# Routed expert slots of a vision-transformer block: up and down matmuls interleaved by chunk, one register load per slot, gathers issued earlier

## The chip, the cores and the metric

The kernel runs on one core of a Trainium2 chip. The metric is device time in microseconds for one execution. A core has five engines that run their own instruction streams and meet at semaphores: PE (matmul; its weight loads are listed as PEld), DVE (elementwise, reductions), ACT (activations, copies), POOL (here gathers, scatters and small arithmetic) and SP (here DMA starts). In the views below PEldq stands for instructions that PE's sequencer carries out itself, such as address arithmetic.

## What is computed

```python
h = tok(x)                                    # patches @ W.T + b, 32 images x 36 patches, width 256
h = concatenate([cls_tok, h])                 # 37 tokens per image, 1184 in all
h = h + attn(layernorm(h))                    # 4 heads, plus a memory read, out projection
...
# ffn(layernorm(h)): one shared expert, and the two best of 8 routed experts
shared = silu(x @ shared_w1.T) @ shared_w2.T                  # 256 -> 1024 -> 256
gate_logits = x @ gate_w.T
top_k_gates, top_k_idx = top_k(gate_logits, 2); top_k_gates = softmax(top_k_gates)
h_e = einsum('td,ehd->teh', x, experts_w1)
expert_out = einsum('teh,edh->ted', silu(h_e), experts_w2)
return h + shared + einsum('ted,te->td', expert_out, gates)
```

## The kernel before

**Stages.** The tokens stand in 11 tiles of 111 (three images each). A front part embeds them and runs attention, software-pipelined over 16 steps. Then comes the shared expert, tile by tile, and meanwhile DVE works out where each token goes. Last come the routed experts as 26 *slots* (`SLOT_TILES`) of 128 rows, each slot for one expert; the rest of this text is on the slots. A tile or slot has a running number `n`, slot `j` being `n = NT + j` with `NT = 11`.

**Precision.** Tokens, hidden values and weights are each split into a high and a low fp16 part, and three products are summed.

**One slot on PE.** `turn` (L559) transposes the slot's gathered rows (4 matmuls, L563) into one PSUM bank. `up` (L567) makes the 1024 hidden values in 8 chunks of 128, each chunk from 6 matmuls of 128 columns (L577, 48 in all); after chunk 3 and chunk 7 it signals `hid_ready` for a half. `down` (L584) brings them back to 256 values: 8 chunks of two matmuls, one of 512 columns (L592) and one of 256 (L594), summed into one bank; it waits for `lo_ready` before chunk 0 and before chunk 4. The weights of all experts lie in SBUF, and which expert a slot uses is known only at run time, so the address of each matmul's weights is computed from a register `base_of[j]`. Four address instructions per `up` chunk and one per `down` chunk, 40 per slot, stand in PE's stream between the matmuls; the order view prints them as ISA, the trace as FUSED_REGOPS.

**Registers.** `know` (L633) fills the registers with one TENSOR_LOAD (L625) of 13 values of `expert_of` (`LOADED = 13`): once before slot 0, and once within slot 12's step, behind its `up`.

**One step.** `slot_step(j)` (L650) has: `up` of slot j, `turn` of slot j+1 (`rows_of`, L637), `down` of slot j-1. For the first slots it also waits until DVE has prepared the weights of the experts that may be needed (`wait_split`).

**The other engines, per slot.** ACT: two `silu` activations (L800, a half each), then `copy_x_t` (L791), which brings the turned rows of the next slot to SBUF, where the next `up` needs them (`x_t_ready`), then up to two conversions of late weight chunks (L730). DVE: `split_hidden` (L1203 high part, L1205 low part, for each half), then `output` of slot j-1 (L1212, L1215: scale by the gate, add the two halves of the bank), then the low part of late weight chunks (L1042; two each in slots 0 to 3, one in 4 and 5). POOL: wait for the slot's result (`y_scaled`) and for the scatter before it (`added`), scatter-add the result to the output (L935), then gather the rows of slot j+4 (L896). Scatters are strictly one after another, since they add into the same rows.

All streams are written out by hand in this order; no scheduler moves anything.

Of the kernel before, what the change touches and what calls it, by code (L numbers as in the profile page):

```python
# [18 lines left out]
ACT = mybir.ActivationFunctionType  # L19
# [6 lines left out]
P = 128  # L26
IMAGES, SEQ, D = 32, 37, 256
PER_TILE = 3
T = PER_TILE * SEQ
NT = -(-IMAGES // PER_TILE)  # L30
# [21 lines left out]
def build(nc, patches, w_embed, embed_bias, w_qk, w_v, w_o, out_bias, betas, mem, z, w_ffn, w_gate,  # L52
# [3 lines left out]
    with ExitStack() as ctx:  # L56
# [233 lines left out]
        def wait_split(eng, chunks):  # L290

            eng.wait_ge(w_lo, chunks)
# [78 lines left out]
        def _(pe):  # L371
# [251 lines left out]
            def experts(first):  # L623

                return nc.values_load_multi_w_load_instructions(  # L625
                    expert_of[0:1, first:min(first + LOADED, SLOT_TILES)],
                    engines=[mybir.EngineType.PE], min_val=EW, max_val=EXPERTS * EW,
                    skip_runtime_bounds_check_because="an expert's number is clamped to 1..EXPERTS where "
                                                      "expert_of is written")[1]

            base_of = {}

            def know(first):  # L633
                for i, value in enumerate(experts(first)):
                    base_of[first + i] = value
# [8 lines left out]
            know(0)  # L644
            wait_split(pe, 2 * CHUNKS)
# [3 lines left out]

            def slot_step(j, r, quad_next):  # L650
# [15 lines left out]
        def _(act):  # L666
# [125 lines left out]

            def silu(n, b, m, first=False):
                for half_ in range(2):
                    act.wait_ge(hid_ready, 2 * n + half_ + 1)
                    if not first:
                        act.wait_ge(lo_ready, 2 * n + half_ - 1)
                    d_ = act_out[:, half_].rearrange("p (a b) -> p a b", b=P)[:, :, 0:m]
                    s_ = bank[2 * b + half_][:].rearrange("p (a b) -> p a b", b=P)[:, :, 0:m]
                    nc.scalar.activation(d_, s_, ACT.Silu,  # L800
                                         scale=1.0 / (X_SCALE * W_SCALE)).then_inc(hid_acted, 1)
# [23 lines left out]
            late_hi(NT - 1)  # L825
            for j in range(len(LATE_SLOT) + len(LATE_SLOT) % 2):
                silu(NT + j, (NT + j) % 2, P)
                copy_x_t(NT + j + 1, (NT + j + 1) % 2, P)
                late_hi(NT + j)
            with act.Fori(len(LATE_SLOT) // 2 + len(LATE_SLOT) % 2, (SLOT_TILES - 2) // 2) as i:  # L830
                for r in range(2):
                    n = 2 * i + r + NT
                    silu(n, (NT + r) % 2, P)
                    copy_x_t(n + 1, (NT + r + 1) % 2, P)
            n = NT + (SLOT_TILES - 2) // 2 * 2
            for n in range(n, NT + SLOT_TILES):
                silu(n, n % 2, P)
                if n + 1 < NT + SLOT_TILES:
                    copy_x_t(n + 1, (n + 1) % 2, P)

        @block.gpsimd
        def _(pool):
# [88 lines left out]
            for j in range(SLOT_TILES):  # L931
                pool.wait_ge(y_scaled, NT + j + 1)
# [5 lines left out]
                if j + 4 < SLOT_TILES:  # L938
                    gather(j + 4)
# [406 lines left out]
```

## Time and profile before

| | us |
|---|---|
| median of 3 runs | 401.28 (400.87 to 401.45) |
| the profiled execution, its own time | 397.15 |
| its span, first to last instruction | 395.4 |
| front part and shared expert, up to slot 1's first matmul | 233.1 |
| slot 1's first matmul to slot 25's first | 141.25 (24 steps) |
| from there to the end of the span | 21.0 |

PE is busy 337.2 us (85%), DVE 255.3, ACT 164.4, POOL 162.3. Busy PE is not PE at its peak: a matmul's recorded duration overlaps the next one's, so starts are to be read, not durations. The chain of waits is the list, in order of time, of what each piece of the last work waited for; "issue" in it is time for which the profile shows no wait.

### The profile page before, as it was taken

Reading aid. Unit: us, or ns where it says so; the run is one execution under the profiler, and the core shown is the slowest. Engines: PE = TensorE matmul, PEld = TensorE weight load, DVE = VectorE, ACT = ScalarE, POOL = GpSimd, SP = SyncE. Lnnn points to the kernel's source line nnn. Section 1 sums busy time; section 2 is a strip of 40 time slices with the busy share of each in tenths; the row PEclk is TensorE's granted clock in tenths of the full one; section 3 lists DMA queues with packets and bytes.
Section 4 is the critical chain, followed back from the end, with each engine's and each line's share of the span. In section 5 each row is a group of like instructions: output and inputs, shape, how many; then the busy total and the mean of one; then the engine's idle time right before and its main releaser. Section 6 shows DMA issues by size and latency. Waiting matters only on the chain.

```text
span 395.4 us, 9873 instructions
## 1 busy us (share of the span) xinstructions
PE 337.2 (85%) x3430; PEld 278.8 (71%) x3430; DVE 255.3 (65%) x559; ACT 164.4 (42%) x371; POOL 162.3 (41%) x232
## 2 busy tenths in 40 slices
PE   4488989889887775499899999999996999999970
PEld 3367878778876563488788788688874887788740
DVE  0156778878684845489998679885563656665640
ACT  1036665675656533534344456542221322332210
POOL 0246575657651212004814312654442444544331
PEclk9699999999996856599999999999998999999995
DMA  7553233343222210634356637322331233323321
GB/s 247 167 183 137 94 98 88 118 130 135 77 78 65 63 37 27 215 121 81 111 118 172 159 87 228 44 47 51 55 56 27 31 54 55 46 39 53 41 28 13
DMA packets 18401, 36.32 MB, mean 92 GB/s; under 512 B 3349, under 2 KB 11000, under 8 KB 18360
## 3 DMA queue, kind: packets, MB, share of 16 engines
q1 hardware_dynamic: 11992, 27.71, 21.9%
q0 software_dynamic: 6368, 8.03, 13.7%
q8 instruction: 29, 0.48, 0.5%
q14 instruction: 12, 0.10, 0.1%
HBM read 28.52 MB, written 7.21 MB: 90 GB/s over the span
## 4 chain that ended last, share of the span: by engine, by line
PE 56%; DVE 17%; POOL 9%; issue 6%; ACT 5%; DMA 5%; SPq 1%; DVEq 0%; POOLq 0%; ACTq 0%
PE bank L577 21%; PE bank L592 13%; PE bank L594 7%; PE bank L454 3%; POOL weights L857 3%; PE bank L491 3%; PE bank L434 2%; DVE weights L1042 2%; DMA weights<-in_out_bias 2%; DVE hid_lo L1205 2%; PE bank L563 2%; PE bank L472 2%; PE bank L462 2%; ACT weights L730 2%; DVE weights L980 2%
## 5 line engine op out<-in xcount | busy, mean ns | idle before, releaser
L577 PEld LDWEIGHTS bank<-x_t,weights 128*128 (+1 forms) x1776 | 102.9, 99 | 8.8 <-issue 1.7
L577 PE MATMUL bank<-x_t,weights 128*128 128x128 f16 (+1 forms) x1776 | 107.3, 220 | 2.0 <-ACT x_t L791 1.9
L592 PE MATMUL bank<-weights,hid_hi 128*128 (+1 forms) x296 | 99.7, 384 | 2.1 <-DVE hid_lo L1205 1.7
L800 ACT ACTIVATE act_out<-bank 128x512 f32<-128x512 f32 (+1 forms) x74 | 42.8, 580 | 128.9 <-PE bank L577 115.3
L594 PE MATMUL bank<-weights,hid_lo 128*128 (+1 forms) x296 | 81.3, 275 | 0.0
L935 POOL DMA_INDIRECT out_rows<-y,add_id x26 | 42.6, 1640 | 79.7 <-DVE y L1215 72.1
L592 PEld LDWEIGHTS bank<-weights,hid_hi 128*128 128x128 f16 (+1 forms) x296 | 32.1, 109 | 31.3 <-issue 1.9
L1205 DVE SCALAR_TENSOR_TENSOR hid_lo<-act_out,hid_hi 128x512 f16<-128x512 f32 (+1 forms) x74 | 50.8, 687 | 2.5
L1203 DVE TENSOR_SCALAR hid_hi<-act_out 128x512 f16<-128x512 f32 (+1 forms) x74 | 37.0, 500 | 23.1 <-ACT act_out L800 22.3
L1042 DVE SCALAR_TENSOR_TENSOR weights<-stage,weights 128x1024 f16<-128x1024 f32 x36 | 43.7, 1227 | 2.4 <-ACT weights L730 2.4
L434 PE MATMUL bank<-weights 128*111 128x256 f32 x132 | 33.2, 405 | 5.6 <-DMA weights<-in_w_embed 5.6
L730 ACT ACTIVATE weights<-stage 128x1024 f16<-128x1024 f32 x36 | 37.4, 1055 | 0.0
L856 POOL TENSOR_SCALAR weights<-weights 111x1 f32<-111x1 f32 x22 | 5.0, 230 | 71.3 <-DVE weights L963 70.9
L594 PEld LDWEIGHTS bank<-weights,hid_lo 128*128 128x128 f16 (+1 forms) x296 | 32.2, 109 | 2.3
L1212 DVE TENSOR_SCALAR y<-bank,slot_gate 128x256 f32<-128x256 f32 x26 | 12.6, 484 | 32.2 <-PE bank L594 31.0
L434 PEld LDWEIGHTS bank<-weights 128*111 128x111 f32 x132 | 24.2, 191 | 11.0 <-DMA weights<-in_w_embed 5.6
L896 POOL DMA_INDIRECT slot_rows<-x_rows,gather_id x26 | 27.7, 1065 | 7.9 <-issue 4.9
L923 POOL DMA_DIRECT2D out_rows<-y x11 | 10.2, 928 | 49.7 <-DVE y L1215 49.7
L454 PE MATMUL bank<-weights 128*128 128x111 f32 x176 | 24.0, 293 | 7.7 <-ACT weights L683 7.6
L454 PEld LDWEIGHTS bank<-weights 128*128 128x128 f32 x176 | 22.2, 204 | 9.3 <-ACT weights L683 8.9
L857 POOL TENSOR_TENSOR weights<-weights 111x1 f32<-111x1 f32 x22 | 24.3, 1107 | 1.8
L791 ACT COPY x_t<-bank 128x512 f16<-128x512 f16 (+1 forms) x37 | 20.9, 564 | 4.1 <-PE bank L563 4.1
(130 smaller groups left out, 448.4 us busy)
## 6 DMA issues: line engine op xcount, KB each, us to landing
stage<-in_w_ffn SPq DMA_DIRECT2D x36, 512.0 KB, 4.7
weights<-in_patches SPq DMA_DIRECT2D x11, 333.0 KB, 3.0
x_rows<-rows SPq DMA_DIRECT2D x11, 111.0 KB
out_rows<-weights SPq DMA_DIRECT2D x10, 111.0 KB
out_rows<-y POOLq DMA_DIRECT2D x10, 111.0 KB, 3.1
weights<-in_w_embed SPq DMA_DIRECT2D x1, 768.0 KB, 4.4
weights<-in_w_qk SPq DMA_DIRECT2D x1, 512.0 KB
slot_rows<-x_rows,gather_id POOLq DMA_INDIRECT x26
```

The source lines that it names most:

```text
L434: mm = nc.tensor.matmul(bank[4][0:T, 0:D], s_patch[:, t % 2, k], s_we[:, k], start=(k == 0), stop=(k == PC - 1))
L454: mm = nc.tensor.matmul(bank[5][:, o * T:(o + 1) * T], s_wqk[:, k, o], xln_t[:, t % 2, k], start=(k == 0), stop=(k == KC - 1))
L577: mm = nc.tensor.matmul(o, weights[:, bass.ds(base + 2 * k * CHUNK + 2 * (col - col % D) + w * D + col % D, P)], x_t[:, b, (2 * x + k) * P ...
L592: nc.tensor.matmul(bank[5 + b][0:m, :], hid_hi[:, b, c * P:c * P + m], weights[:, bass.ds(at, 2 * D)], start=(c == 0), stop=False)
L594: mm = nc.tensor.matmul(bank[5 + b][0:m, 0:D], hid_lo[:, b, c * P:c * P + m], weights[:, bass.ds(at, D)], start=False, stop=(c == HC - 1))
L730: nc.scalar.mul(hi_of(c), staged_of(c), W_SCALE).then_inc(w_hi, 1)
L800: nc.scalar.activation(d_, s_, ACT.Silu, scale=1.0 / (X_SCALE * W_SCALE)).then_inc(hid_acted, 1)
L857: link(nc.gpsimd.tensor_tensor(y_, v_, half[0:T, 0:1], ALU.pow))
L935: nc.gpsimd.indirect_dma_start(out=out, out_offset=bass.IndirectOffsetOnAxis(ap=add_id[:, j:j + 1], axis=0), in_=y[:, (NT + j) % 2], in_of ...
L1042: nc.vector.scalar_tensor_tensor(out=lo_of(c), in0=staged_of(c), scalar=W_SCALE, in1=hi_of(c), op0=ALU.mult, op1=ALU.subtract).then_inc(w_ ...
L1203: nc.vector.tensor_scalar(four(hid_hi), src, H_SCALE, None, ALU.mult).then_inc(hi_ready, 1)
L1205: nc.vector.scalar_tensor_tensor(out=four(hid_lo), in0=src, scalar=H_SCALE, in1=four(hid_hi), op0=ALU.mult, op1=ALU.subtract).then_inc(lo_ ...
```

## The change

On PE a slot step no longer runs all of `up`, then `turn`, then all of `down`. It runs up chunk c of slot j, then down chunk c of slot j-1, for c from 0 to 7 (`up_chunk`, `down_chunk`), with `turn` of slot j+1 and the register load of slot j+1 between up chunk 4 and down chunk 4. `know` loads one value: two loads before slot 0, then one in each of the steps 1 to 24. On ACT the copy of the next slot's rows stands between the two activations of a slot instead of behind them, with the weight conversions behind the second. On POOL the gather of slot j+4 stands ahead of the wait for slot j's result. DVE and SP are as before.

```diff
-LOADED = 13
...
+            def know(j):
+
+                base_of[j] = nc.values_load_multi_w_load_instructions(
+                    expert_of[0:1, j:j + 1], engines=[mybir.EngineType.PE], min_val=EW, max_val=EXPERTS * EW,
...
             know(0)
+            know(1)
             wait_split(pe, 2 * CHUNKS)
             up(NT, NT % 2, P, base_of[0])
             rows_of(1, 1, 0)
             down(NT - 1, 0, T, 0)
...
             def slot_step(j, r, quad_next):
 
+                this_expert, last_expert = base_of[j], base_of[j - 1]
                 if j < EXPERTS:
                     wait_split(pe, (j + 2) * CHUNKS)
-                up(NT + j, (NT + r) % 2, P, base_of[j])
-                if (j + 1) % LOADED == 0 and j + 1 < SLOT_TILES:
-                    know(j + 1)
-                if quad_next is not None:
-                    rows_of(j + 1, (r + 1) % 4, quad_next)
-                down(NT + j - 1, (NT + r + 1) % 2, P, base_of[j - 1])
+                n, b = NT + j, (NT + r) % 2
+                pe.wait_ge(x_t_ready, n + 1)
+                for c in range(HC):
+                    up_chunk(n, b, P, this_expert, c)
+                    if c == 4 and quad_next is not None:
+                        rows_of(j + 1, (r + 1) % 4, quad_next)
+                        know(j + 1)
+                    down_chunk(n - 1, 1 - b, P, last_expert, c)
...
+            def slot_act(n, b):
+                silu_half(n, b, P, 0)
+                copy_x_t(n + 1, 1 - b, P)
+                silu_half(n, b, P, 1)
...
             for j in range(SLOT_TILES):
+                if j + 4 < SLOT_TILES:
+                    gather(j + 4)
                 pool.wait_ge(y_scaled, NT + j + 1)
                 if j:
                     pool.wait_ge(added, 16 * j)
                 nc.gpsimd.indirect_dma_start(
...
-                if j + 4 < SLOT_TILES:
-                    gather(j + 4)
```

PE, before, in the step of slot 12: the end of its `up` (L577), the load of 13 values, the turning of slot 13's rows, and the start of `down` of slot 11.

```order
L577 ISA
L577 MATMUL bank<-x_t,weights 128x128
L625 TENSOR_LOAD expert_of
L563 MATMUL bank<-id,slot_rows 128x128 [waits slot_rows_in1]
L563 MATMUL bank<-id,slot_rows 128x128 x3
L592 ISA [waits lo_ready]
L592 MATMUL bank<-weights,hid_hi 128x512
L594 MATMUL bank<-weights,hid_lo 128x256
L592 ISA
L592 MATMUL bank<-weights,hid_hi 128x512
L594 MATMUL bank<-weights,hid_lo 128x256
```

PE, now, in the step of slot 1 (all steps to 24 read alike): the end of up chunk 4 (L651), the turning of slot 2's rows (L562), the load of one value (L626), down chunk 4 of slot 0 (L664, L666), and the start of up chunk 5.

```order
L651 ISA
L651 MATMUL bank<-x_t,weights 128x128
L562 MATMUL bank<-id,slot_rows 128x128 [waits slot_rows_in2]
L562 MATMUL bank<-id,slot_rows 128x128 x3
L626 TENSOR_LOAD expert_of
L664 ISA [waits lo_ready]
L664 MATMUL bank<-weights,hid_hi 128x512
L666 MATMUL bank<-weights,hid_lo 128x256
L651 ISA
L651 MATMUL bank<-x_t,weights 128x128 x2
L651 ISA
L651 MATMUL bank<-x_t,weights 128x128
```

The load moved from one place with 13 values to 24 places with one value each, between the turning and a wait for `lo_ready`; the number of address instructions and matmuls per slot is the same.

ACT, before, in slot 1: both activations (L800), the copy (L791), the weight conversions (L730), and the first of slot 2.

```order
L800 ACTIVATE act_out<-bank 128x512 [waits lo_ready,hid_ready] x2
L791 COPY x_t<-bank 128x512 [waits hid_ready,x_turned]
L730 ACTIVATE weights<-stage 128x4x256 [waits stage_in4]
L730 ACTIVATE weights<-stage 128x4x256 [waits stage_in5]
L800 ACTIVATE act_out<-bank 128x512 [waits lo_ready,hid_ready] x2
```

ACT, now, in slot 1: the activations are L823, the copy L815, the conversions L754.

```order
L823 ACTIVATE act_out<-bank 128x512 [waits lo_ready,hid_ready]
L815 COPY x_t<-bank 128x512 [waits hid_ready,x_turned]
L823 ACTIVATE act_out<-bank 128x512 [waits lo_ready,hid_ready]
L754 ACTIVATE weights<-stage 128x4x256 [waits stage_in4]
L754 ACTIVATE weights<-stage 128x4x256 [waits stage_in5]
```

The copy moved ahead of the second activation.

POOL, before, at the start of the slots: the last write of the shared expert (L923), the first scatter (L935), the gather of slot 4 (L896), the second scatter.

```order
L923 DMA out_rows<-y 74x256 [waits y_scaled]
L935 DMA out_rows<-y,add_id 1312x256 [waits dummy_out,shared_out2,y_scaled,shared_out1,shared_out0]
L896 DMA slot_rows<-x_rows,gather_id 128x512 [waits x_turned]
L935 DMA out_rows<-y,add_id 1312x256 [waits added,y_scaled]
L896 DMA slot_rows<-x_rows,gather_id 128x512 [waits x_turned]
```

POOL, now, at the same place (L950 the shared expert's write, L923 the gather, L964 the scatter).

```order
L950 DMA out_rows<-y 74x256 [waits y_scaled]
L923 DMA slot_rows<-x_rows,gather_id 128x512 [waits dummy_out,shared_out2,x_turned,shared_out1,shared_out0]
L964 DMA out_rows<-y,add_id 1312x256 [waits y_scaled]
L923 DMA slot_rows<-x_rows,gather_id 128x512 [waits x_turned]
L964 DMA out_rows<-y,add_id 1312x256 [waits added,y_scaled]
```

Each gather moved ahead of one scatter.

## Rows read from the trace of the kernel before

**Rows 1.** Chain that ended last: start us, us, what.

```profile
251.06 2.68 PE bank L577 x48
...
295.98 2.77 PE bank L577 x48
298.75 3.33 issue
...
312.31 2.85 PE bank L577 x48
```

**Rows 2.** Timeline, PE and ACT, one slot step: start us, us, engine line operation.

```profile
346.09 2.93 PE L577 MATMUL bank<-x_t,weights 128*128 128x128 f16 x48
348.86 0.39 PE L563 MATMUL bank<-id,slot_rows 128*128 128x128 f16 x4
349.08 0.38 PE L592 MATMUL bank<-weights,hid_hi 128*128 x1
...
351.68 0.50 PE L577 MATMUL bank<-x_t,weights 128*128 128x128 f16 x6
...
349.18 0.60 ACT L800 ACTIVATE act_out<-bank 128x512 f32<-128x512 f32 x1 [0.88 <-PE bank L577]
349.68 0.58 ACT L791 COPY x_t<-bank 128x512 f16<-128x512 f16 x1
```

**Rows 3.** Lines L577, L592: duration ns min/median/max, first and last start us.

```profile
L577 PEldq FUSED_REGOPS  x32: 42/46/46, 344.6 to 348.7; - x32
...
L592 PEldq FUSED_REGOPS  x8: 46/46/46, 348.8 to 349.8; - x8
...
L577 PEldq FUSED_REGOPS  x32: 42/46/46, 350.3 to 354.4; - x32
```

**Rows 4.** Line L625, and L577, L592 around its second load.

```profile
L625 PEldq TENSOR_LOAD <-expert_of x2: 1469/2428/3386, 224.3 to 298.6; - x2
...
L577 PEldq FUSED_REGOPS  x32: 42/46/46, 294.3 to 298.4; - x32
...
L592 PEldq FUSED_REGOPS  x8: 46/46/46, 302.1 to 303.0; - x8
```

**Rows 5.** Windows: PE, PEld, DVE, ACT, POOL busy, PEclk, DMA share, GB/s.

```profile
302.10:305.50 3.40, 3.40 (x14) 1.78 (x15) 0.00 (x0) 0.58 (x1) 0.00 (x0) 0.50 0.00 1
...
237.20:242.80 5.60, 5.60 (x70) 4.50 (x68) 5.50 (x9) 3.60 (x6) 0.09 (x1) 1.00 0.81 241
```

**Rows 6.** Timeline, PE and POOL, around slot 3.

```profile
227.01 3.46 PE L577 MATMUL bank<-x_t,weights 128*128 128x128 f16 x48
...
242.71 1.73 POOL L935 DMA_INDIRECT out_rows<-y,add_id  x1 [7.27 <-DVE y L1215]
244.74 1.04 POOL L896 DMA_INDIRECT slot_rows<-x_rows,gather_id  x1 [0.30 <-issue]
247.86 1.69 POOL L935 DMA_INDIRECT out_rows<-y,add_id  x1 [2.08 <-DMA out_rows<-y,add_id]
248.06 0.40 PE L563 MATMUL bank<-id,slot_rows 128*128 128x128 f16 x4 [0.79 <-DMA slot_rows<-x_rows,gather_id]
```

**Rows 7.** Timeline, DVE, ACT and POOL, the last slots.

```profile
377.41 0.60 ACT L800 ACTIVATE act_out<-bank 128x512 f32<-128x512 f32 x1 [0.91 <-PE bank L577]
378.50 0.69 DVE L1205 SCALAR_TENSOR_TENSOR hid_lo<-act_out,hid_hi 128x512 f16<-128x512 f32 x1
380.15 0.48 DVE L1212 TENSOR_SCALAR y<-bank,slot_gate 128x256 f32<-128x256 f32 x1 [0.96 <-PE bank L594]
381.43 1.55 POOL L935 DMA_INDIRECT out_rows<-y,add_id  x1 [3.96 <-DVE y L1215]
385.91 1.55 POOL L935 DMA_INDIRECT out_rows<-y,add_id  x1 [2.93 <-DMA out_rows<-y,add_id]
```

**Rows 8.** Timeline, PE, the first up matmuls of slots 1 and 25.

```profile
233.12 0.55 PE L577 MATMUL bank<-x_t,weights 128*128 128x128 f16 x7
...
374.37 0.61 PE L577 MATMUL bank<-x_t,weights 128*128 128x128 f16 x8
```

More of the change, by code:

```diff
@@ L621, in _ @@
             up(NT - 1, 0, T, 0)
[L623 to L627, printed above, removed]
+            base_of = {}
+            def know(j):
+                base_of[j] = nc.values_load_multi_w_load_instructions(
+                    expert_of[0:1, j:j + 1], engines=[mybir.EngineType.PE], min_val=EW, max_val=EXPERTS * EW,
                     skip_runtime_bounds_check_because="an expert's number is clamped to 1..EXPERTS where "
[L629 to L635, printed above, removed]
+                                                      "expert_of is written")[1][0]
             def rows_of(j, r, quad):
@@ L648, in _, with up_chunk, down_chunk @@
             down(NT - 1, 0, T, 0)
+            def up_chunk(n, b, m, base, c):
+                o = bank[2 * b + c // 4][:, c % 4 * P:c % 4 * P + m]
+                col = c * P
+                for k in range(KC):
+                    for w, x in ((0, 0), (0, 1), (1, 0)):
+                        mm = nc.tensor.matmul(
+                            o, weights[:, bass.ds(base + 2 * k * CHUNK + 2 * (col - col % D)
+                                                  + w * D + col % D, P)],
+                            x_t[:, b, (2 * x + k) * P:(2 * x + k) * P + m],
+                            start=(k == 0 and w + x == 0), stop=(k == 1 and w == 1))
+                if c % 4 == 3:
+                    mm.then_inc(hid_ready, 1)
+            def down_chunk(n, b, m, base, c):
+                if c % 4 == 0:
+                    pe.wait_ge(lo_ready, 2 * n + c // 4 + 1)
+                at = base + 2 * KC * CHUNK + c * 2 * D
+                nc.tensor.matmul(bank[5 + b][0:m, :], hid_hi[:, b, c * P:c * P + m],
+                                 weights[:, bass.ds(at, 2 * D)], start=(c == 0), stop=False)
+                mm = nc.tensor.matmul(bank[5 + b][0:m, 0:D], hid_lo[:, b, c * P:c * P + m],
+                                      weights[:, bass.ds(at, D)], start=False, stop=(c == HC - 1))
+                if c == HC - 1:
+                    mm.then_inc(y_ready, 1)
             def slot_step(j, r, quad_next):
+                this_expert, last_expert = base_of[j], base_of[j - 1]
                 if j < EXPERTS:
                     wait_split(pe, (j + 2) * CHUNKS)
[L654 to L659 removed]
+                n, b = NT + j, (NT + r) % 2
[6 more added lines that the diff above has]
+                    down_chunk(n - 1, 1 - b, P, last_expert, c)
             for j in range(1, SLOT_TILES):
@@ L791, in copy_x_t, with silu_half @@
                 nc.scalar.copy(d_[:, :, 0:m], v_[:, :, 0:m]).then_inc(x_t_ready, 1)
+            def silu_half(n, b, m, half_, first=False):
+                act.wait_ge(hid_ready, 2 * n + half_ + 1)
+                if not first:
+                    act.wait_ge(lo_ready, 2 * n + half_ - 1)
+                d_ = act_out[:, half_].rearrange("p (a b) -> p a b", b=P)[:, :, 0:m]
+                s_ = bank[2 * b + half_][:].rearrange("p (a b) -> p a b", b=P)[:, :, 0:m]
+                nc.scalar.activation(d_, s_, ACT.Silu,
+                                     scale=1.0 / (X_SCALE * W_SCALE)).then_inc(hid_acted, 1)
             def silu(n, b, m, first=False):
                 for half_ in range(2):
[L795 to L801, printed above, removed]
+                    silu_half(n, b, m, half_, first)
             copy_x_t(0, 0, T, first=True)
@@ L831, in _ @@
                 for r in range(2):
[L832 to L839, printed above, removed]
+                    slot_act(2 * i + r + NT, (NT + r) % 2)
+            for n in range(NT + (SLOT_TILES - 2) // 2 * 2, NT + SLOT_TILES - 1):
+                slot_act(n, n % 2)
+            silu(NT + SLOT_TILES - 1, (NT + SLOT_TILES - 1) % 2, P)
         @block.gpsimd
```

3 lines of the change are left out of this document (1 added, 2 removed).

## Prediction

> **What bounds the kernel now.** I read first the chain of waits for the slots, then windows for PE's clock, the timeline of one step, and last the sequencer's own instructions, since the chain ends on PE without saying what holds PE.
>
> The change touches nothing ahead of slot 0's `up`, so 227 us of the span stay. From slot 1's first matmul to slot 25's are 374.37 - 233.12 = 141.25 us for 24 steps [rows 8]. Within it two places stand out. The second load of 13 values leaves PE without work for 3.33 us [rows 1], and behind it the granted clock is 0.50, the 1.2 GHz level, from 302.1 to 305.5 [rows 5]. The two steps from 295.98 to 312.31 take 16.33 us [rows 1]. And once PE waits 0.79 us for gathered rows [rows 6]. The other 22 steps take (141.25 - 16.33 - 0.79) / 22 = 5.64 us each.
>
> What fills 5.64? One step [rows 2]: `up` from 346.09 to 348.86 is 2.77, turning 0.22, `down` from 349.08 to 351.68 is 2.60. The shortest `up` in the chain takes 2.68 [rows 1]. So PE by itself would need 2.68 + 0.22 + 2.60 = 5.50: only 0.14 per step is to be had from PE's side.
>
> The sequencer is nearly as full. Its address instructions for `up` start at 344.6 and 348.7, 31 intervals, about 0.13 each, although each is recorded as 46 ns; with those of `down` the 40 run from 344.6 to 349.8 [rows 3]. One more interval of 0.12 and it could start the next slot at 349.9, so its work is about 5.3 per step. It starts at 350.3, because the first address waits for `x_t_ready`, and the copy ends at 349.68 + 0.58 = 350.26 [rows 2, 3]. So the loop that sets the step is: copy done, 4.1 us of addresses for `up`, turning at its end, second activation (from 349.18, 0.60), copy (0.58), 350.3. PE, sequencer and this loop lie within 0.35 us of each other.
>
> **The change part by part.**
>
> *Copy between the activations, turning behind chunk 4.* The loop loses the second activation and the three chunks behind the turning. The copy is then done about 0.22 + 0.1 + 0.58 = 0.9 us after chunk 4, while up chunks 5 to 7 and down chunks 4 to 7 take 3 x 0.34 + 4 x 0.325 = 2.3 us: x_t is off the path, with 1.4 us of cover. The loop bound of 5.64 falls to the larger of PE's 5.50 and the sequencer's time. That is what is late next.
>
> *Interleaving itself.* Same matmuls, same 40 address instructions. Between the long matmuls of `down` (0.325 a pair, from 2.60 / 8) the short ones no longer run dry at the end of `up`; this is within the 0.14. The new waits: down chunk 4 needs the low parts of the second half, whose matmuls end one down chunk before the step's end. From the activation's start at 377.41 to the end of the low part at 378.50 + 0.69 is 1.8 us [rows 7], plus 0.2 to start: 2.0. It is needed 5 up chunks and 5 down chunks later, 3.3 us: covered by 1.3. The first half has the same distance. Behind a late wait the whole of PE's stream would stand, but I see none late in steps of 5.5 and more.
>
> *One load per slot, the part that decides.* Call the load of one value X. The two loads of 13 values took 1.469 and 3.386 us [rows 4], and nothing in the rows explains the difference. No row has a load of one value. Lower bound, if all is per value: 1.469 / 13 = 0.11. The same from the second: 3.386 / 13 = 0.26. Upper bound, if all is fixed: 1.469, or 3.386 for the second. A load also takes the sequencer around it: step 12's 40 addresses run from 294.3 to 303.0, 8.7 [rows 4], against 5.2 [rows 3], so 3.5 for a load of 3.386, about 0.15 more. The sequencer then needs S = 5.3 + 0.15 + X = 5.45 + X per step, and with nothing that blocks it, this is the step if it exceeds 5.50. I take X = 0.26, since the second load is the one that was made in the slots, among scatters and gathers: S = 5.71.
>
> The rows give a per-value price only if there is no fixed part. The Trainium skill bears on this twice. "Runtime: NRT & Kernel Launch", section on instruction fetch mechanics, puts a register load (from HBM there) at about 200 ns per register even in bulk; both loads here agree roughly (113 and 260). With X = 0.20 the sum below would give 1.4 us less. "DMA: Bandwidth & Descriptors", section on latency, gives `tensor_load` a floor of about 600 ns; no row here shows one, and with it the sum would be +5.4 instead of -2.8. That rule speaks against the change.
>
> *The load of 13 within slot 12's step goes*, and with it the idle time and the low clock: this is inside the 141.25, which I replace whole by 24 S. So is the wait of 0.79 for rows: the gather of slot 4 is now issued ahead of the first scatter, which started at 242.71, where it was issued at 244.74 [rows 6]; with every gather one scatter earlier this wait has 2 us of room and more.
>
> *First load.* `up` of slot 0 takes 3.46 [rows 6] against 2.93 [rows 2], as the sequencer comes late from its load of 1.469; two loads of one value take less: -0.5 (0 to -0.6).
>
> *Early slots.* DVE is busy 5.50 of 5.60 us there [rows 5], with two weight conversions. The second half and the output now come later in its stream's time, so its chunk conversions fall just ahead of the next first half. I book +0.6 for four steps (0 to 2).
>
> *Gathers and scatters.* The order of the two kinds stays alternating; POOL's pair of 1.73 + 0.30 + 1.04 lies beside the rest. The chain scatter to scatter is 247.86 - 242.71 = 5.15 [rows 6], below any S here: hidden, by 0.4 at the least.
>
> *Tail.* Before, slot 24's result is scattered 4.02 us after slot 25's last activation started (381.43 - 377.41) [rows 7]. Now down of 24 is interleaved, so that activation starts later by seven down chunks, 7 x 0.325 = 2.28; then low part done (379.19, 1.78), and from the output's start to the scatter 381.43 - 380.15 = 1.28: 2.28 + 3.06 = 5.34, 1.3 later. The last scatter follows 4.48 later, behind the one ahead (385.91 - 381.43) as now. +1.3.
>
> **Sum.** Change = 24 S - 141.25 + 1.3 - 0.5 + 0.6 = 24 S - 139.85. With S = 5.71: 137.04 - 139.85 = -2.8. The profiled execution's own 397.15 would become 394.4; the median of the runs is 4.1 above that execution, and I keep this distance: 401.28 - 2.8 = 398.5. The change is zero at S = 5.83, X = 0.38. What a measurement tells from no change is about 0.2%, 0.8 us.
>
> **Rivals.**
>
> 1. *The load has a fixed part* (slower). One mechanism: the sequencer stands still 24 times for X, and nothing hides it, since it has no spare time beyond 0.2 us per step. It decides from X = 0.38. If a third of the cheaper load is fixed, X = 0.49 + 0.98 / 13 = 0.57: +24 x 0.31 = +7.4 against the forecast, 405.9. For it: the two loads of equal size differ by 1.9 us, so the price isn't simply per value. Against: nothing shows a fixed part.
> 2. *Nearly all of it is fixed*, X = 1.469: S = 6.92, +29.0, 427.5 (were it 3.386, it would be over 470; I leave that out of the range).
> 3. *The load is at its cheapest*, X = 0.11: S = 5.56, against PE's 5.50, nearly all of what is there: 24 x 5.56 - 139.85 = -6.4, 394.9. I count this to the forecast's own range (394.5 to 400.4).
> 4. *No change*: X between 0.34 and 0.41, the gains at slot 12 paid back in small coin: 400.5 to 402.1.
> 5. *It doesn't do what it says*: DVE's late low parts hold PE in every step, not only in the first. For it: output of slot j-1 stands behind the second half. Against: later slots have no conversions on DVE, and both covers are above 1 us. If they failed by 0.3 a step: +7.2, 405.7.
>
> **How the numbers follow.** Forecast with rival 3: 0.48. No change: 0.08. A fixed part up to X = 0.9: 0.31. Above: 0.08. DVE: 0.05. So faster by over 0.2%: 0.48; within: 0.08; slower: 0.44. Both signs hold much; the forecast's own range is 394.5 to 400.4. The range for 8 in 10 reaches from 394 (X = 0.11 and a tail that costs less) to 413 (X = 0.86).
>
> **What would show it.** The duration of the 24 loads of one value is the first thing to read: at 0.26 I am right, at 0.4 and more I am wrong. Slot steps of 5.7, with no gap of 3.3 us and a full clock at slot 12. The address instructions should run without a pause from step to step (no wait for the copy), with short matmuls spread apart by it. No wait of PE for gathered rows, and the last scatter about 1.3 later against slot 25's first matmul. Wrong would be: steps of 5.5 though X exceeds 0.1, which would say that the sequencer isn't the limit; or waits for low parts in later steps.

## The result, and the profile after

The changed kernel takes 393.15 us (median of 4 runs, 392.73 to 393.42), and the kernel before took 401.07 beside it (398.58 to 401.45). The ratio is 0.9845, with a 95% interval of 0.9803 to 0.9886; on the 401.28 of the start that is 395.1. The change makes the kernel faster by 1.5%, where 398.5 was forecast. The profiled executions differ less: 397.15 before, 393.42 after, and their spans are 395.4 and 391.6. The working below goes by the spans, since it is there that places can be read.

The page after, its first lines and its row of the granted clock (40 slices of the span). PE's busy time is the same as before (338.3 against 337.2).

```profile
span 391.6 us, 9897 instructions
## 1 busy us (share of the span) xinstructions
PE 338.3 (86%) x3430; PEld 279.4 (71%) x3430; DVE 248.3 (63%) x559; ACT 166.7 (43%) x371; POOL 162.1 (41%) x232
...
PEclk9799999999996855579999999999999999999995
```

The clock row has no dent behind the middle of the slots any more: it answers to the window at 0.50 in [rows 5]. Windows from slot 11 to slot 16 of the changed kernel say the same (columns as in [rows 5]): PE is busy throughout and the granted clock is 1.00, the 2.4 GHz level.

```profile
293.00:300.00 7.00, 7.00 (x88) 5.56 (x86) 3.83 (x8) 2.81 (x5) 3.74 (x3) 1.00 0.26 40
300.00:320.00 20.00, 20.00 (x243) 15.81 (x241) 10.61 (x21) 6.03 (x11) 9.15 (x8) 1.00 0.34 54
```

The loads, and then the address instructions of one late step (lines of the sequencer: ns min/median/max, first and last start). They answer to [rows 4] and [rows 3].

```profile
L626 PEldq TENSOR_LOAD <-expert_of x26: 297/301/607, 225.2 to 366.6; - x26
...
L651 PEldq FUSED_REGOPS  x32: 42/46/46, 340.9 to 346.3; - x32
...
L651 PEldq FUSED_REGOPS  x32: 42/46/46, 346.5 to 351.9; - x32
```

A load of one value takes 0.30, the first one 0.607. The addresses of the next step start at 346.5, 0.2 behind the last `up` address of this one, with one address of `down` (L664) between them, so there is no pause. Before, half a microsecond lay between [rows 3], where the sequencer waited for the copy. The timeline of ACT and PE in the same step (answers to [rows 2]):

```profile
343.85 0.50 PE L651 MATMUL bank<-x_t,weights 128*128 128x128 f16 x6
...
344.19 0.39 PE L562 MATMUL bank<-id,slot_rows 128*128 128x128 f16 x4
...
344.69 0.58 ACT L815 COPY x_t<-bank 128x512 f16<-128x512 f16 x1 [0.29 <-PE bank L562]
```

The copy ends at 345.27, and the first address that needs it starts at 346.5: x_t has 1.2 us of cover, where 1.4 was predicted.

The start of slot 0's `up` [rows 6], the first matmuls of the slots 1, 2 and 25 [rows 8], and the last slots [rows 7], from the timeline:

```profile
227.86 3.05 PE L576 MATMUL bank<-x_t,weights 128*128 128x128 f16 x48
...
233.57 0.50 PE L651 MATMUL bank<-x_t,weights 128*128 128x128 f16 x6
...
239.07 0.50 PE L651 MATMUL bank<-x_t,weights 128*128 128x128 f16 x6
...
369.40 0.50 PE L651 MATMUL bank<-x_t,weights 128*128 128x128 f16 x6
...
374.62 0.60 ACT L823 ACTIVATE act_out<-bank 128x512 f32<-128x512 f32 x1 [2.08 <-PE bank L651]
...
377.59 1.55 POOL L964 DMA_INDIRECT out_rows<-y,add_id  x1 [3.78 <-DVE y L1242]
...
382.19 1.55 POOL L964 DMA_INDIRECT out_rows<-y,add_id  x1 [3.05 <-DMA out_rows<-y,add_id]
```

Cut at these matmuls the two spans compare as follows.

| us | before | after | difference |
|---|---|---|---|
| up to slot 1's first matmul | 233.12 | 233.57 | +0.45 |
| 24 steps, slot 1 to slot 25 | 141.24 | 135.83 | -5.41 |
| from there to the end | 20.99 | 22.21 | +1.22 |
| span | 395.35 | 391.61 | -3.74 |

### The profile page after: what moved, and what is told of

Same layout as the page of the kernel before. It is cut to its first block, busy times and chain, and to the rows that moved or that the text cites. A ratio compares the mean times of both kernels' runs of the same rounds, so it can differ in the third digit from the quotient of the medians.

```text
span 391.6 us, 9897 instructions
## 1 busy us (share of the span) xinstructions
PE 338.3 (86%) x3430; PEld 279.4 (71%) x3430; DVE 248.3 (63%) x559; ACT 166.7 (43%) x371; POOL 162.1 (41%) x232
## 4 chain that ended last, share of the span: by engine, by line
PE 60%; DVE 15%; POOL 9%; issue 5%; ACT 5%; DMA 4%; SPq 1%; ACTq 0%; POOLq 0%; DVEq 0%
PE bank L651 17%; PE bank L664 12%; PE bank L666 6%; PE bank L576 5%; PE bank L453 3%; POOL weights L884 3%; PE bank L591 3%; PE bank L433 3%; PE bank L490 2%; DMA weights<-in_out_bias 2%; PE bank L562 2%; PE bank L471 2%; ACT weights L754 2%; DVE weights L1007 2%; DVE hid_lo L1232 1%
## 5 line engine op out<-in xcount | busy, mean ns | idle before, releaser
L651 PEld LDWEIGHTS bank<-x_t,weights 128*128 x1200 | 84.0, 98 | 25.9
L651 PE MATMUL bank<-x_t,weights 128*128 128x128 f16 x1200 | 99.6, 219 | 0.0
L823 ACT ACTIVATE act_out<-bank 128x512 f32<-128x512 f32 (+1 forms) x74 | 42.8, 580 | 118.7 <-PE bank L651 82.8
L664 PE MATMUL bank<-weights,hid_hi 128*128 x200 | 76.3, 381 | 0.1
L964 POOL DMA_INDIRECT out_rows<-y,add_id x26 | 42.8, 1645 | 73.5 <-DVE y L1242 65.1
L1230 DVE TENSOR_SCALAR hid_hi<-act_out 128x512 f16<-128x512 f32 (+1 forms) x74 | 31.8, 430 | 57.1 <-ACT act_out L823 54.7
L666 PE MATMUL bank<-weights,hid_lo 128*128 x200 | 54.5, 273 | 0.0
L433 PE MATMUL bank<-weights 128*111 128x256 f32 x132 | 35.0, 421 | 5.8 <-DMA weights<-in_w_embed 5.8
L754 ACT ACTIVATE weights<-stage 128x1024 f16<-128x1024 f32 x36 | 37.3, 1052 | 0.0
L576 PE MATMUL bank<-x_t,weights 128*128 128x111 f16 (+1 forms) x576 | 32.9, 220 | 1.9 <-ACT x_t L815 1.9
L576 PEld LDWEIGHTS bank<-x_t,weights 128*128 128x128 f16 (+1 forms) x576 | 31.7, 102 | 3.3 <-issue 1.5
L591 PE MATMUL bank<-weights,hid_hi 128*111 128x512 f16 (+1 forms) x96 | 32.0, 380 | 2.2 <-DVE hid_lo L1232 1.7
L923 POOL DMA_INDIRECT slot_rows<-x_rows,gather_id x26 | 27.4, 1054 | 10.2 <-issue 7.6
L950 POOL DMA_DIRECT2D out_rows<-y x11 | 10.2, 928 | 49.6 <-DVE y L1242 49.6
L593 PE MATMUL bank<-weights,hid_lo 128*111 128x256 f16 (+1 forms) x96 | 26.2, 273 | 0.0
```

Source lines behind the costliest of these rows:

```text
L433: mm = nc.tensor.matmul(bank[4][0:T, 0:D], s_patch[:, t % 2, k], s_we[:, k], start=(k == 0), stop=(k == PC - 1))
L576: mm = nc.tensor.matmul(o, weights[:, bass.ds(base + 2 * k * CHUNK + 2 * (col - col % D) + w * D + col % D, P)], x_t[:, b, (2 * x + k) * P ...
L591: nc.tensor.matmul(bank[5 + b][0:m, :], hid_hi[:, b, c * P:c * P + m], weights[:, bass.ds(at, 2 * D)], start=(c == 0), stop=False)
L651: mm = nc.tensor.matmul(o, weights[:, bass.ds(base + 2 * k * CHUNK + 2 * (col - col % D) + w * D + col % D, P)], x_t[:, b, (2 * x + k) * P ...
L664: nc.tensor.matmul(bank[5 + b][0:m, :], hid_hi[:, b, c * P:c * P + m], weights[:, bass.ds(at, 2 * D)], start=(c == 0), stop=False)
L666: mm = nc.tensor.matmul(bank[5 + b][0:m, 0:D], hid_lo[:, b, c * P:c * P + m], weights[:, bass.ds(at, D)], start=False, stop=(c == HC - 1))
```

## The experiments

All experiments are compared on the same cut, in us. PE's sequencer runs ahead of its matmuls, and steps counted by the matmuls leave out what of this lead is used up on the way; so the fifth column, and the expectations that give the 24 steps, count on the sequencer: from slot 1's first instruction there, a wait for weights that stands 0.11 ahead of its first address, to slot 25's first address. The last column is the median of the later steps counted by addresses; by matmuls the interleaved kernels without a load in the slots, and interleaved_quads, have 5.50 there.

| kernel | to slot 1 | 24 steps, matmuls | tail | 24 steps, addresses | late step |
|---|---|---|---|---|---|
| before | 233.12 | 141.24 | 20.99 | 141.24 | 5.66 |
| before_again | 233.36 | 142.23 | 20.98 | 142.32 | 5.66 |
| after | 233.57 | 135.83 | 22.21 | 137.23 | 5.65 |
| after_again | 234.06 | 135.82 | 21.97 | 137.24 | 5.65 |
| old_order_one_value | 232.01 | 139.62 | 20.83 | 139.43 | 5.80 |
| interleaved_no_load | 235.90 | 132.53 | 22.02 | 132.94 | 5.50 |
| interleaved_early_load | 235.98 | 132.51 | 21.84 | 132.87 | 5.50 |
| interleaved_two_registers | 232.95 | 144.15 | 22.15 | 145.56 | 6.03 |
| interleaved_quads | 233.47 | 132.76 | 22.02 | 133.54 | 5.3, with a load 5.8 |
| late_gather | 232.90 | 139.49 | 22.15 | 140.90 | 5.65 |
| interleaved_early_aligned | 233.70 | 132.89 | 22.08 | 133.30 | 5.53 |
| old_order_quads | 233.03 | 139.60 | 20.93 | 139.64 | 5.65, with a load 5.9 |
| old_act_order | 234.29 | 167.01 | 22.52 | 168.43 | 6.95 |

Theory A throughout: PE's sequencer sets the changed kernel's step, with about 5.3 of addresses and the load of one value on top, all of it in the open. Theory B: PE's matmuls or DVE's low parts set it, and the load lies beside them.

### The changed kernel once more (after_again)

No edit.

> The changed kernel once more, as the base for the other runs on the same chip. Both theories: span about 391.6 us, slot steps 5.65, loads of one value 0.30 us, about 1.5% faster than before.

The median is 393.07 (6 runs) against 397.67 for the kernel before (18 runs), ratio 0.9901 (0.9861 to 0.994). The span is 391.8 and the 24 steps take the same as in the first trace to a hundredth. The gain is there again, but smaller in ratio, and it is the time of before that moved: see before_again.

### No load in the slots (interleaved_no_load)

```diff
-            know(0)
-            know(1)
+            know(0, 13)
+            know(13, 13)
...
-                        know(j + 1)
```

Here `know(first, count)` loads `count` values at once.

> The changed kernel with all 26 values loaded ahead of slot 0 (13 and 13), none in the slot steps. Theory A (the sequencer is the limit of the changed kernel's steps): steps fall from 5.65 to PE's own 5.55, 24 x 0.1 = 2.4 us less, less up to 1.5 for the second load ahead of slot 0: span 389.2 to 390.7. Theory B (a load of 0.3 us is hidden behind queued matmuls): no change in the steps, span 391.6 to 393.

The late steps take 5.50, where theory A has 5.55. One step, from its turning to the next one (the timeline):

```profile
338.39 0.39 PE L562 MATMUL bank<-id,slot_rows 128*128 128x128 f16 x4
...
343.90 0.39 PE L562 MATMUL bank<-id,slot_rows 128*128 128x128 f16 x4
```

Taking the load out of the step removes 0.15 of 5.65, half of its 0.30. That fits a step that goes from the sequencer (5.65) to PE's own 5.50: below that, the load's absence can't be seen. But the time is 392.45 (7 runs), ratio 0.9901 (0.9867 to 0.9936), no better than the changed kernel: the loads cost it ahead of slot 0.

```profile
L626 PEldq TENSOR_LOAD <-expert_of x2: 1479/2300/3122, 223.9 to 225.4; - x2
```

Both loads stand in a row, 4.6 us in all, and slot 1 starts at 235.90, 2.3 later than in the changed kernel.

### A second load per slot (interleaved_two_loads, interleaved_two_registers)

```diff
                         know(j + 1)
+                        know(j + 1)
```

> The changed kernel with each load of one value made twice. Theory A (sequencer-bound): every step longer by what one load takes in the sequencer's stream, 0.24 to 0.30 us: 24 x 0.27 = 6.5 us more, span about 398. Theory B (hidden): span 391.6.

This told nothing about the load: the build drops a register that nobody reads, and the trace has 26 loads, not 50. It is a third measurement of the changed kernel: 392.15 (6 runs), ratio 0.9884 (0.9849 to 0.9919), 24 steps 137.25. The next kernel reads both: `down` takes its address from a register of its own.

```diff
+                down_of[j] = nc.values_load_multi_w_load_instructions(
+                    expert_of[0:1, j:j + 1], ...)[1][0]
...
-                this_expert, last_expert = base_of[j], base_of[j - 1]
+                this_expert, last_expert = base_of[j], down_of[j - 1]
```

> The changed kernel with two loads of one value in every slot step, into two registers that are both used (up takes one, down the other), so that both stay in the program; the run interleaved_two_loads turned out to be the changed kernel itself, since the builder had dropped the unused register. Theory A (sequencer-bound steps): every step longer by one load, 0.24 to 0.30 us: the 24 steps take 137.24 + 24 x 0.27 = 143.7 (143.0 to 144.4). Theory B (hidden): 137.2.

```profile
L626 PEldq TENSOR_LOAD <-expert_of x26: 297/303/596, 223.9 to 374.3; - x26
L630 PEldq TENSOR_LOAD <-expert_of x25: 301/307/308, 224.6 to 368.6; - x25
```

And its timeline, from one turning to the next:

```profile
344.31 0.39 PE L562 MATMUL bank<-id,slot_rows 128*128 128x128 f16 x4
345.02 0.39 PE L668 MATMUL bank<-weights,hid_hi 128*128 x1 [0.32 <-issue]
...
350.34 0.39 PE L562 MATMUL bank<-id,slot_rows 128*128 128x128 f16 x4
350.97 0.39 PE L668 MATMUL bank<-weights,hid_hi 128*128 x1 [0.24 <-issue]
```

A step is 6.03 long, and PE now stands idle behind the turning with "issue" as its only releaser. The 24 steps grow by 145.56 - 137.24 = 8.3, which is 0.35 per load, and the late ones by 6.03 - 5.65 = 0.38. So theory A holds, B (no growth) falls, and the price was even higher than A's upper end of 144.4 (145.56): a load costs its recorded 0.30 and about 0.08 around it. The sequencer without any load then needs about 5.65 - 0.38 = 5.27. The single run gave 401.06, 8 more than the changed kernel.

The same place shows the price on PE. From the start of the turning to the next matmul of `down` it is 0.22 in the late steps without a load (median), 0.32 in the changed kernel and 0.69 with two loads. The load stands right behind the turning, and PE has only the four matmuls of the turning to do meanwhile. No run puts a single load at another place of the step, so whether it would be hidden there stays open.

### Old order, one value per slot (old_order_one_value)

```diff
-LOADED = 13
+LOADED = 1
...
-                if (j + 1) % LOADED == 0 and j + 1 < SLOT_TILES:
-                    know(j + 1)
                 if quad_next is not None:
                     rows_of(j + 1, (r + 1) % 4, quad_next)
+                    know(j + 1)
```

> The kernel before with only the register load changed: one value per slot, behind the turning; up, turn and down in whole blocks, ACT and POOL as before. Theory A (what was gained is the stall at the load of 13 values and the low clock behind it; the step was held by the loop through the copy, and the sequencer had 0.3 us of slack in it): steps stay at 5.64 in spite of the load, the dent of 5.05 us at slot 12 is gone, span 395.4 - 5.0 = 390.4, as fast as the changed kernel or faster. Theory B (interleaving is what earns, and pays for the loads): without it steps of 5.64 + 0.24 = 5.88, span 395.4 - 5.0 + 5.7 = 396.1.

The median is 395.62 (12 runs), ratio 0.9958 (0.9935 to 0.9982). The steps take 5.80, between the 5.64 of a hidden load and the 5.88 of an open one. The lines of the sequencer in one step, then the turning, the first matmul of `down` and the copy (from the timeline):

```profile
L577 PEldq FUSED_REGOPS  x32: 42/46/46, 312.0 to 316.1; - x32
L592 PEldq FUSED_REGOPS  x8: 46/46/46, 316.7 to 317.5; - x8
L577 PEldq FUSED_REGOPS  x32: 42/46/46, 317.7 to 321.9; - x32
```

```profile
316.28 0.39 PE L563 MATMUL bank<-id,slot_rows 128*128 128x128 f16 x4
316.75 0.39 PE L592 MATMUL bank<-weights,hid_hi 128*128 x1
...
316.98 0.58 ACT L791 COPY x_t<-bank 128x512 f16<-128x512 f16 x1
```

The copy ends at 317.56 and no longer sets the step. In the kernel before, from slot 7 on, each slot's first address starts 0.04 behind the copy's end, and 0.4 to 0.6 behind the last address of `down`. Here, in the same steps, it starts 0.08 to 0.20 behind the copy, and 0.13 to 0.26 behind the last address of `down` (317.5 and 317.7 in the lines above). The load is in the open on PE instead: `down` starts 0.47 behind the turning, where it was 349.08 - 348.86 = 0.22 [rows 2]. PE's own 5.50 becomes about 5.75, and 5.80 was measured. Theory A had the load inside the loop's slack on the sequencer and did not ask what PE does meanwhile. The split of the change, by matmuls: the load moved alone gives 141.24 - 139.62 = 1.6 of the 24 steps (the two traces of the kernel before differ by 1.0 there), and interleaving with the new places of the copy and the gather gives 139.62 - 135.83 = 3.8 on top of it.

### The activations in the old order (old_act_order)

```diff
                 silu_half(n, b, P, 0)
-                copy_x_t(n + 1, 1 - b, P)
                 silu_half(n, b, P, 1)
+                copy_x_t(n + 1, 1 - b, P)
```

> The changed kernel with ACT's order as before (both activations, then the copy). Theory A (the copy is on the path unless it stands between the activations): the copy ends about 1.4 us behind the last up chunk, where the next step's first matmul is due 0.3 behind it, and the sequencer starts its addresses only then: steps of 6.6 to 6.8 us, 24 steps 158 to 163. Rival (the order on ACT doesn't matter, since ACT is idle half of the time): 137.2.

```profile
344.06 0.50 PE L651 MATMUL bank<-x_t,weights 128*128 128x128 f16 x6
344.60 0.60 ACT L823 ACTIVATE act_out<-bank 128x512 f32<-128x512 f32 x1 [2.35 <-PE bank L651]
345.09 0.58 ACT L815 COPY x_t<-bank 128x512 f16<-128x512 f16 x1
...
345.81 0.60 PE L651 MATMUL bank<-x_t,weights 128*128 128x128 f16 x6 [0.92 <-ACT x_t L815]
```

The timeline around the end of a step: the second activation waits for up chunk 7, which is now almost the last thing in the step, and the copy waits for the activation; PE stands idle for 0.92 and its sequencer starts the next slot's 40 addresses only then. A step takes 6.95, the run 425.66, 32 more than the changed kernel and more than the 158 to 163 that was expected for the 24 steps. Without the copy's place between the activations interleaving loses here.

### The gather in its old place (late_gather)

```diff
             for j in range(SLOT_TILES):
-                if j + 4 < SLOT_TILES:
-                    gather(j + 4)
...
+                if j + 4 < SLOT_TILES:
+                    gather(j + 4)
```

> The changed kernel with the gather of slot j+4 back behind the scatter of slot j. Theory A: the gather has to be there one step's up chunk 4 later; only the first ones are late, where PE had waited 0.79 us before: 24 steps 137.2 to 138.2. Theory B (gathers are late in every step, since the output comes later in the step than before): PE waits for rows in many steps, 24 steps 142 or more.

The 24 steps take 140.90, between the two theories, and one wait does most of it. The waits of PE for rows, from 238 to 256:

```profile
PE bank L562 <- DMA slot_rows<-x_rows,gather_id: 2.6, 1, 2.6
```

POOL in the same place:

```profile
244.10 1.73 POOL L962 DMA_INDIRECT out_rows<-y,add_id  x1 [8.88 <-DVE y L1242]
...
246.13 1.04 POOL L923 DMA_INDIRECT slot_rows<-x_rows,gather_id  x1 [0.31 <-issue]
```

The interleaved order makes slot 0's result later: the first scatter starts at 244.10, not at 242.71 [rows 6], and the gather of slot 4 behind it at 246.13, while the turning now comes four chunks earlier in its step. The wait of 0.79 grows to 2.6, and slot 3's step to 8.80 from 5.93. Slot 5's step waits once more, 0.23, and takes 6.26 instead of 5.73; later ones don't wait. The 24 steps grow by 140.90 - 137.23 = 3.7 in all, and the single run gave 396.35. So the earlier gather is worth more within this change than the 0.79 that it removes.

### All loads ahead of the slots (interleaved_early_load, interleaved_early_aligned)

```diff
             inverse()
+            pe.wait_ge(experts_known, 1)
+            know(0, 13)
...
-            know(0)
-            know(1)
+            know(13, 13)
...
-                        know(j + 1)
```

> The changed kernel with the 26 values loaded ahead of the slots, 13 behind the matmuls of inverse() in the shared expert's stage and 13 behind down of tile 9; no load in the slot steps. Both loads of 13 stand where PE's sequencer has matmuls queued ahead. Theory A (slot steps are set by PE's sequencer): the 24 steps take 133 us as in the run without loads in the slots, against 137.24, and the start of slot 1 isn't delayed by the 2 us that two loads in a row cost there: span 388, the fastest so far. Theory B (steps were shorter there for another reason): 24 steps at 137.

The median is 391.93 (4 runs), ratio 0.9824 (0.9772 to 0.9875), span 390.3 instead of 388. The first load is hidden in the shared expert, but the second one takes 3.39, as before in slot 12, though no scatter or gather is near it:

```profile
L619 PEldq TENSOR_LOAD <-expert_of x2: 1297/2343/3389, 200.3 to 225.2; - x2
```

So its place among the slots isn't why it is slow. What the three slow ones (3.39 in the kernel before, 3.12 and 3.39) share is that they start at value 13; the fast ones start at 0. From this came a new theory, F: four values that start at a multiple of four are read at once. The edit moves the cut only:

```diff
-            know(0, 13)
+            know(0, 16)
...
-            know(13, 13)
+            know(16, 10)
```

> The changed kernel with the 26 values loaded ahead of the slots, 16 behind inverse() and 10 behind down of tile 9, cut at multiples of four. Theory F (four values that begin at a multiple of four are read at once, at 0.33 us, others one by one at 0.26 to 0.30): the loads take 4 x 0.33 = 1.3 and 2 x 0.33 + 0.54 = 1.2 us, against 1.30 and 3.39 in interleaved_early_load; slot 1 then starts 2 to 2.6 us earlier than there by this cause, 24 steps 132.9, span about 388. Rival (the price goes by count alone): the second load takes 2.6 us, the first 4.2.

```profile
L619 PEldq TENSOR_LOAD <-expert_of x2: 1296/1299/1302, 199.6 to 225.1; - x2
```

16 values take 1.30, and ten values from 16 on take 1.30 too (1.2 expected), so F holds against the rival, which had 4.2 and 2.6. The only slow start among the runs is 13; which other starts are slow was not tried. Slot 1 starts at 233.70, and the 24 steps take 132.89. The median is 390.51 (390.06 to 391.25, 4 runs) against 400.22, ratio 0.976 (0.9705 to 0.9815): with a span of 388.7 it is 3 us shorter than the changed kernel, since all that the load took from the steps is now off them. Only the single run of interleaved_quads below is as fast.

### Four values every fourth slot (interleaved_quads, old_order_quads)

```diff
-                        know(j + 1)
+                        if (j + 1) % 4 == 0:
+                            know(j + 1, 4)
```

> The changed kernel with loads of 4 values, ahead of slot 0 and in every fourth step. Measures a load's price by size: if the price is a value's 0.30 us each, a load takes 1.2; if a start and then less, 0.6 to 0.9. Theory A (sequencer-bound): three of four steps at 5.50, the fourth longer by the load; 24 steps together 132.9 + 6 x 1.0 = 139 at most, 136 if a load of four takes 0.6. Theory B (hidden): 24 steps 133.

```profile
L626 PEldq TENSOR_LOAD <-expert_of x7: 333/334/627, 225.1 to 357.2; - x7
```

Four values cost 0.33, about what one costs, and only six steps have a load. The 24 steps take 133.54, below the 136 to 139 of theory A's expectation: PE stays at 5.50 a step even where the sequencer has a load, since its other steps are shorter than PE's and give the lead back. The kernel has 3.7 less than the changed one, and the single run gave 390.06 with a span of 388.3, the level of interleaved_early_aligned. The same loads in the old order (the edit of old_order_one_value with `LOADED = 4` and its condition kept):

> The kernel before with loads of four values behind the turning, in every fourth step; nothing else changed. It takes away only the long load at slot 12 and the low clock behind it. If this was the main part of the gain: 24 steps 141.24 - 5.05 = 136.2 (plus up to 0.4 for each of 6 loads, so 136.2 to 138.5), span 391 to 393; steps without a load stay at 5.64, as the loop through the copy holds them. If the whole-block order costs nothing by itself: 24 steps like the interleaved one with loads of four, 133.5.

The median is 395.74 (4 runs), ratio 0.9884 (0.9822 to 0.9947). Its 24 steps take 139.64, over the expected 136.2 to 138.5; 1.7 of that is a wait for gathered rows, which the earlier gather of the change would have removed:

```profile
PE bank L563 <- DMA slot_rows<-x_rows,gather_id: 1.7, 1, 1.7
```

With cheap loads in both, interleaving with its earlier gather is worth 139.64 - 133.54 = 6.1 in the steps (6.8 by matmuls), and gives 1.1 back in the tail.

### The kernel before once more (before_again)

No edit.

> The kernel before, a second trace. Its runs scatter over some 6 us, those of the changed kernel over 3. If the place at slot 12 scatters (load of 13 values, and how long the clock stays at its lower level behind it), the two steps there take another time than 16.3 us here, up to 3 us more, since the clock's spells in the traces are multiples of 3.4 us. If it is the front part, the 24 steps take 141.2 again and the time up to slot 1 differs from 231.6.

```profile
L625 PEldq TENSOR_LOAD <-expert_of x2: 1482/2447/3412, 224.5 to 299.5; - x2
```

The single run gave 398.41 with a span of 396.6. The load of 3.4, the two long steps at slot 12 (9.11 and 7.34) and 3.4 us of clock at the 1.2 GHz level are the same in both traces. So slot 12 isn't why the kernel before ranges from 394.7 to 402.7 over all runs, where the changed one has 391.8 to 394.9. Early steps and the front part differ by 0.2 to 1 between the two traces; neither of the explanations that I had is supported, and the cause of that scatter stays open. It is also why the ratio of the pair stands between 0.9845 and 0.9901 from chip to chip.

## Why the prediction was right

The direction held, and so did what the prediction said of the step: the loop through the copy before, the sequencer after, the stall at slot 12 gone. The size did not. On the comparable time -2.8 was forecast and -6.2 measured, more than twice as much (398.5 against 395.1); with the ratio of after_again it would be -4.0. On the spans it is -2.8 against -3.74. With the measured load of 0.30 in place of 0.26 the prediction's own sum gives 24 x 5.75 - 139.85 = -1.9, further off, so the terms around the load matter as much as the load. Point by point:

- **What bounds the step.** Right. The loop through the copy set 5.64; the sequencer set it afterwards, and PE's own 5.50 came out to the hundredth in interleaved_no_load. Of the 5.64, interleaving with the copy's new place gives 0.14, and one load takes 0.15 back. Slot steps are as long as before, and **all of the gain is elsewhere**: 16.33 - 2 x 5.64 = 5.05 at slot 12 (the idle 3.33 and the low clock behind it) and the 0.79 of the gather.
- **The load, X.** Forecast 0.26, measured 0.30. The prediction put 0.15 around it and 5.3 under it; interleaved_two_registers gives 0.08 and 5.27. (The 0.15 was read too high in its own rows: 3.5 for a load of 3.386 is 0.11.) S came out at 5.65 instead of 5.71: two terms too high by 0.07 and 0.03, one too low by 0.04. That is 24 x 0.06 = 1.4 of the difference.
- **Why X was near 0.26.** Half by luck. I took the second load's 3.386 / 13 since it was made among scatters and gathers. The early loads show that its surroundings did nothing: it starts at a value that isn't a multiple of four and is priced as if its values were read one by one, which is why its price per value is near that of single loads. The rivals 1 and 2 with a fixed part (0.57 and 1.469) fall; what looks like one is 0.3 on the first load only (0.607). The Trainium skill's "DMA: Bandwidth & Descriptors", section on latency, gives a floor of about 600 ns for `tensor_load`: the first load agrees with it, the 25 others, at 0.30, do not, and by it the changed kernel would have been slower. "Runtime: NRT & Kernel Launch", section on instruction fetch mechanics, says about 200 ns per register, for loads from HBM. Here the values lie in SBUF, and it is 0.30 for a single one and 0.33 / 4 = 0.08 in fours, on either side of it. The two loads of 13, which the prediction called in rough agreement with it, lie at 0.113 and 0.260 per value, and no one price per register fits all of these.
- **The lead of the sequencer.** Missed. At slot 1 the sequencer of the changed kernel is 1.78 ahead of PE, at slot 4 only 0.2, and at slot 25 0.38. While that lead lasts, PE runs at its own 5.50 (239.07 - 233.57), and the sequencer's longer step is not paid for. Counted by matmuls, the steps are 137.23 - 1.40 = 135.83. In the kernel before the lead is 1.5 at both ends, since its sequencer waits for the copy in each step, so nothing of it is used up. This is another 1.4.
- **Early steps.** Booked at +0.6. By the addresses it is 137.23 - 24 x 5.65 = 1.6. Slots 1 to 4 are slow on the sequencer, slot 3 with 6.40 the most. There the prediction's reason for its +0.6 can be seen: DVE, behind two weight conversions, is late with a low part, and the sequencer waits for it before the first chunk of `down`. The addresses of `down` (L664) between 243 and 245.2, and the timeline of DVE:

```profile
L664 PEldq FUSED_REGOPS  x2: 46/46/46, 243.6 to 245.0; - x2
```

```profile
244.28 0.69 DVE L1232 SCALAR_TENSOR_TENSOR hid_lo<-act_out,hid_hi 128x512 f16<-128x512 f32 x1
```

  The low part ends at 244.97, and the address that waits for it starts at 245.01, 0.77 behind the one ahead of it instead of 0.12. That is 0.65, about what was booked. Most of the other 1.0 is slot 1's step of 6.28, in which the sequencer has its full lead and stands several times for 0.1 to 0.2 with nothing that the trace shows it to wait for; its cause stays open. The three differences give the 1.8 by which the 24 steps beat the prediction (-5.41 against 24 x 5.71 + 0.6 - 141.25 = -3.6).
- **First load.** Slot 0's `up` takes 3.05 instead of 3.46: -0.41, where -0.5 was booked. The front part as a whole is 0.45 longer all the same, since the first load already starts 0.85 later (225.17 against 224.32), and slot 0 with it. Nothing in the change touches what lies ahead of that load, and slot 1's first address stands anywhere from 230.2 to 232.8 in traces of kernels that are alike up to it. The first load starts at 223.6 to 225.7 in three traces of the changed kernel and at 224.3 and 224.5 in the two of the kernel before, so this is scatter and no effect of the change. It gives back 0.95 of the 1.8 (-0.5 booked, +0.45 measured).
- **Gather.** Right in that no wait for rows is left, and short of the truth in its worth: late_gather shows 3.7, not 0.79, once the order is interleaved.
- **Tail.** Predicted +1.3, measured +1.22. The activation starts 374.62 - 369.40 = 5.22 behind slot 25's first matmul, where it was 377.41 - 374.37 = 3.04: later by 2.18 (2.28 predicted). From it to slot 24's scatter is 377.59 - 374.62 = 2.97 (3.06 predicted, 4.02 before), and the last scatter follows 4.60 later (4.48 before).
- **Low parts of DVE (rival 5).** Not in every step: the trace shows no wait of PE from 255 to 369, and without a load the steps reach 5.50. The mechanism itself is there once, in slot 3's step (above, under early steps).

## What to carry to other kernels

Before moving a register load in or out of a loop, look at whether the sequencer or the engine sets the step, count its address instructions by their distance and not by their duration, and put the loads where they hold up nothing: taking them out of the slots gave 3 us more than spreading them over the slots. Load registers in fours from a multiple of four. When two orders of an engine are interleaved, move the other engines' work in the same step with them, as one copy behind the wrong activation cost 32 us here and one gather behind the wrong scatter 3.7.

## What the runs showed of the hardware

- A register load is cheap by fours and dear by ones: 0.333 for 4 values at a multiple of four, 1.30 for 16 from 0, 1.30 for 10 from 16, 1.3 to 1.5 for 13 from 0, but 3.1 to 3.4 for 13 from 13, and 0.30 for a single one, wherever it stands in the value list (one of them, in slot 1 of old_order_one_value, took 0.42). The first load ahead of slot 0 takes 0.3 more where it has one value or four (0.60 to 0.63); of 16 values at 199.6 it isn't to be seen.
- An address instruction of PE's sequencer is recorded with 46 ns but the next one starts 0.12 to 0.13 later, so 40 of them fill about 5.3 of a step in which PE itself needs 5.50. A load in this stream costs about 0.08 more than its record.
- A gap of 3.3 us in PE's work was followed by 3.4 us at the 1.2 GHz level in both traces of the kernel before, and no trace of a kernel without this gap has a lower clock among the slots. PE's wait of 2.6 in late_gather was followed by a granted clock of 1.00.
